# A macaron block with linear attention: the reciprocal denominators go to the channels by DMA and multiply A.v's output instead of q, the key sums of all groups stand in the scores' buffer, and the engines' orders are rewritten

## The reference

```
x = x + 0.5 * ffn(layernorm(x))
x = x + attn(layernorm(x))
x = x + 0.5 * ffn(layernorm(x))          # the same ffn weights

ffn:  s = x @ Win + bin            # 512 -> 64
      g = sum_i relu(s * W1[:, i] + b1[:, i]) * W2[:, i] + b2     # 16 inner units
      out = g @ Wout + bout        # 64 -> 512
attn: q, k, v = split(x @ w_attn)  # 512 -> 3 * 512, 16 heads of 32 channels
      q = elu(q) + 1;  k = elu(k) + 1
      S_t = S_{t-1} + k_t v_t^T;   z_t = z_{t-1} + k_t          # per head, causal
      y_t = (q_t S_t) / (q_t . z_t + 1e-6)
      out = y @ w_proj
```

## Time and profile before

| | |
|---|---|
| runs, median of 3 | 2411.91 us |
| profiled execution, its own time | 2411.75 us |
| its span | 2410.0 us |
| TensorE matmul busy | 2315.7 us (96%) |
| weight loads | 1796.5 us (75%) |
| VectorE, ScalarE, GpSimd busy | 79%, 59%, 34% |
| mean granted clock, share of full | 0.985 |

### The profile page before, as it was taken

How to read it: one execution, slowest core, us unless ns; L and a number is a source line. 1 busy time by engine, 2 the same in 40 slices (tenths; PEclk the granted TensorE clock), 3 DMA queues, 4 the chain that set the end, 5 groups by cost and what they waited for, 6 DMA issues and landing times.

```text
span 2410.0 us, 76110 instructions
## 1 busy us (share of the span) xinstructions
PE 2315.7 (96%) x33474; PEld 1796.5 (75%) x33474; DVE 1898.9 (79%) x3346; ACT 1424.5 (59%) x2267; POOL 824.3 (34%) x869
## 2 busy tenths in 40 slices
PE   3999999999999999999999999999999999999995
PEld 3777777777777777777777777777777777777774
DVE  6678887788887778887788887788878778887756
ACT  5556556556566556666556656555656655655644
POOL 6223333333333333333233333323233333333211
PEclk7999999999999999999999999999999999999997
DMA  5001101111101111101111100111100111100000
GB/s 171 1 2 36 35 4 37 37 37 37 37 2 37 36 37 37 37 2 37 37 37 37 37 18 21 37 37 37 37 20 19 37 37 37 36 20 2 19 19 36
DMA packets 39355, 76.98 MB, mean 32 GB/s; under 512 B 4081, under 2 KB 4081, under 8 KB 39026
## 3 DMA queue, kind: packets, MB, share of 16 engines
q1 hardware_dynamic: 39026, 72.12, 8.7%
HBM read 38.56 MB, written 33.55 MB: 30 GB/s over the span
## 4 chain that ended last, share of the span: by engine, by line
PE 67%; DVE 11%; POOL 8%; issue 5%; ACT 4%; DMA 3%; SPq 1%; DVEq 0%; POOLq 0%
PE bank L978 28%; PE att L978 14%; PE att L1081 5%; PE att L1106 5%; POOL z L347 4%; POOL res L339 3%; PE bank L1012 2%; PE att L1012 2%; PE att L996 2%; DVE z L721 2%; DVE st L649 2%; PE att L1097 2%; PE bank L1070 2%; PE att L1051 1%; PE bank L1021 1%
## 5 line engine op out<-in xcount | busy, mean ns | idle before, releaser
L439 ACT ACTIVATE xhat<-res,nmr,rstd 128x512 f32<-128x512 f32 x384 | 301.1, 808 | 287.4 <-DVE nmr L657 235.5
L454 ACT ACTIVATE ffr<-ffs,b1c,w1c 128x512 f32<-128x512 f32 (+1 forms) x544 | 425.5, 810 | 6.4 <-DVE acc_psum L684 3.2
L684 DVE SCALAR_TENSOR_TENSOR acc_psum<-ffr,w2c,acc_psum 128x512 f32<-128x512 f32 (+1 forms) x510 | 382.2, 750 | 33.7 <-ACT ffr L454 11.0
L351 POOL TENSOR_SCALAR_AFFINE_SELECT A<-A 128x512 f32<-128x512 f32 x256 | 157.1, 638 | 614.5 <-ACT A L416 614.5
L347 POOL TENSOR_TENSOR z<-qT,z 128x512 f32<-128x512 f32 x128 | 201.8, 1587 | 470.0 <-DVE zc L726 227.6
L339 POOL TENSOR_TENSOR res<-res,hbout 128x512 f32<-128x512 f32 x256 | 323.7, 1287 | 4.0 <-ACT xhat L439 3.4
L649 DVE BATCH_NORM_STATS2 st<-res 128x6 f32<-128x512 f32 x384 | 259.7, 676 | 20.5 <-DMA res<-in_L_attn_x_dram 15.2
L746 DVE TENSOR_TENSOR A<-att,tri 128x512 f32<-128x512 f32 x256 | 166.4, 681 | 58.2 <-PE att L1081 57.2
L978 PE MATMUL att<-xh,wa_h 128*128 128x512 f32 x524 | 207.0, 395 | 0.0
L978 PE MATMUL att<-xl,wa_h 128*128 128x512 f32 x524 | 207.0, 395 | 0.0
L978 PE MATMUL att<-xh,wa_l 128*128 128x512 f32 x524 | 207.0, 395 | 0.0
(11 more groups left out here) (129 smaller groups left out, 5133.1 us busy)
## 6 DMA issues: line engine op xcount, KB each, us to landing
res<-in_L_attn_x_dram SPq DMA_DIRECT2D x32, 1024.0 KB, 5.5
out_dram<-res SPq DMA_DIRECT2D x32, 1024.0 KB, 4.3
kT<-in_L_attn_w_attn_dram SPq DMA_DIRECT2D x1, 1024.0 KB, 5.3
qT<-in_L_attn_w_attn_dram SPq DMA_DIRECT2D x1, 1024.0 KB, 10.7
v<-in_L_attn_w_attn_dram SPq DMA_DIRECT2D x1, 1024.0 KB, 14.1
A<-in_L_attn_w_proj_dram SPq DMA_DIRECT2D x4, 256.0 KB, 13.1
win<-in_L_ffn_Win_dram SPq DMA_DIRECT2D x4, 128.0 KB, 8.0
z<-in_L_ffn_Wout_dram SPq DMA_DIRECT2D x2, 128.0 KB, 7.7
```

The source lines that it names most:

```text
L351: eng.affine_select(out=A[:, h, :, :], in_=A[:, h, :, :], compare_op=ALU.is_ge, fill=0.0, base=0, pattern=[[0, 4], [1, P]], channel_multip ...
L439: eng.activation(xhat[t % 2][:, :], res[b % SLOTS][:, t, :], ACT.Identity, bias=nmr[:, n, b % 2, t:t + 1], scale=rstd[:, n, b % 2, t:t + 1 ...
L454: eng.activation(ffr[i % 2][p, :], ffs[p, :], ACT.Relu, bias=b1c[p, i:i + 1], scale=w1c[p, i:i + 1]).then_inc(s_hr, 1)
L684: eng.scalar_tensor_tensor(psum[p, :], r[p, :], w2c[p, i:i + 1], psum[p, :], ALU.mult, ALU.add).then_inc(s_hm, 1)
```

## The change

- `spread` leaves TensorE, with `chans_of` and `qnorm`. SP now writes the reciprocals to a scratch tensor in DRAM (four DMAs of 16 x 128), waits for them, waits for this turn's `ff_in` and for `ynorm` of the block before, and reads them back with four DMAs, each of which puts 8 KB (4 heads x 512 tokens) into every one of a group's 32 partitions. They land in `rs`, which is the memory of `xf[1]`, the transposed input of the first ffn.
- `ynorm` (VectorE, four of them) multiplies A.v's output in `att` by `rs`, in place, before `ysplit`.
- `scores` waits for elu + 1 of q and k alone. The running sums of all four groups stand in `A` (`z4`) instead of two alternating buffers, so a `zsum` waits for no `den`; `score` and `mask`, which write `A`, wait for all of `den`.
- `ktok` has two halves, so a `key` copy waits for the `update` before the last.
- The orders of TensorE, VectorE, ScalarE and GpSimd, and the bank table, are rewritten.

```diff
+            def spread(b):                                  # SP
+                e.wait_ge(s_rec, b + 1)
+                for t in range(TILES):
+                    eng.dma_start(scratch[b % 2, :, t, :], rden[D * t:D * t + 16, :]).then_inc(s_rw, 16)
+                e.wait_ge(s_rw, 64 * (b + 1))
+                e.wait_ge(s_fi, b + 2)
+                e.wait_ge(s_yn, 4 * b)
+                for g in range(4):
+                    eng.dma_start(rs[D * g:D * g + D, :, :].rearrange("d h n -> d (h n)"),
+                                  scratch[b % 2, 4 * g:4 * g + 4].rearrange("h t n -> (h t n)").unsqueeze(0)
+                                  .to_broadcast([D, 4 * BLK])).then_inc(s_rs, 16)
...
-            def qnorm(b, t):                                # VectorE
-                w = slice(t * P, t * P + P)
-                e.wait_ge(s_rb, b + 1)
-                eng.tensor_tensor(qT[:, :, w], att[:, t, :].rearrange("p (g i) -> p g i", g=4), qT[:, :, w],
-                                  ALU.mult).then_inc(s_qn, 1)
+            def ynorm(b, t):
+                e.wait_ge(s_num, 4 * b + t + 1)
+                e.wait_ge(s_rs, 64 * (b + 1))
+                eng.tensor_tensor(att[:, :, 0:P], att[:, :, 0:P], rs[:, :, t * P:t * P + P], ALU.mult).then_inc(s_yn, 1)
...
-                e.wait_ge(s_den, 4 * b + g - 1)             # zsum, VectorE
+                e.wait_ge(s_num, 4 * b)
+                e.wait_ge(s_walo, 4)
...
-                e.wait_ge(s_qn, 4 * b + t + 1)              # scores, TensorE
+                for which in range(2):
+                    e.wait_ge(s_elu[which], 4 * b + 4)
...
-                e.wait_ge(s_num, 4 * b + t + 1)             # ysplit, ScalarE
+                e.wait_ge(s_yn, 4 * b + t + 1)
...
-                e.wait_ge(s_up, nth_update(b, t) - 1)       # key, ScalarE
+                e.wait_ge(s_up, nth_update(b, t) - 2)
```

More of the change, by code:

```diff
@@ L274, in _ @@
             load(4)
[L275 to L280, removed]
+            for j in range(NB + 1):
+                if on(j):
+                    spread(j)
+                if on(j - 1):
+                    store(j - 1)
+                    if on(j - 1 + SLOTS):
+                        load(j - 1 + SLOTS)
             for b in range(NB - SLOTS, NB):
@@ L394, in _ @@
                 if on(j - 1):
+                    bias(0, j - 1, 1)
+                    bias(0, j - 1, 2)
                     bias(0, j - 1, 3)
                 if on(j):
+                    mask(j, 3, 0)
                     mask(j, 3, 2)
[L398 to L404, removed]
                     rstds(L3, j)
@@ L629, in _ @@
                     channels(j + 1, 3)
-                if on(j) and updates(j, 3):
-                    key(j, 3)
                 if on(j):
@@ L872, in _ @@
                 if on(j - 1) or on(j + 2):
-                    hidden(j, 6)
+                    hidden(j, 7)
+                if on(j + 1):
+                    channels(j + 1, 0)
                 if on(j):
@@ L878, in _ @@
                 if on(j - 1) or on(j + 2):
-                    hidden(j, 7)
                     hidden(j, 8)
+                if on(j):
+                    update(j, 1)
+                    ynorm(j, 1)
+                if on(j - 1) or on(j + 2):
                     hidden(j, 9)
                 if on(j):
-                    update(j, 1)
                     ysplit(j, 1)
-                    outer(j, 0)
-                    mask(j, 2, 3)
-                    mask(j, 2, 1)
-                if on(j + 1):
-                    channels(j + 1, 0)
                 if on(j - 1) or on(j + 2):
@@ L910, in _ @@
                     ysplit(j, 3)
+                if on(j) and updates(j, 3):
+                    update(j, 3)
                 if on(j + 1):
                     channels(j + 1, 2)
-                if on(j + 3):
-                    shift(L1, j + 3)
-                if on(j):
-                    outer(j, 2)
-                if on(j + 1):
-                    channels(j + 1, 3)
                 if on(j - 1) or on(j + 2):
@@ L1157, in _ @@
                 if on(j):
-                    den(j, 0)
-                    den(j, 1)
-                    key(j, 0)
                     values(j, 1, 0)
@@ L1164, in _ @@
                 if on(j):
-                    den(j, 2)
-                    den(j, 3)
+                    key(j, 0)
                     values(j, 1, 1)
-                    spread(j)
+                    scores(j, 0)
                     values(j, 2, 0)
                     values(j, 2, 1)
-                    scores(j, 0)
-                    key(j, 1)
                     values(j, 3, 0)
                     attend(j, 0)
-                    update(j, 0)
-                    values(j, 3, 1)
-                    scores(j, 1)
-                    key(j, 2)
-                    outer(j, 0, 0)
-                    attend(j, 1)
-                    update(j, 1)
-                    outer(j, 0, 1)
-                    scores(j, 2)
                 if on(j + 1):
@@ L1186, in _ @@
                 if on(j):
-                    outer(j, 1, 0)
-                    attend(j, 2)
-                    update(j, 2)
-                    outer(j, 1, 1)
-                    scores(j, 3)
+                    values(j, 3, 1)
+                    key(j, 1)
+                    scores(j, 1)
+                    update(j, 0)
+                    update(j, 1)
+                    key(j, 2)
+                if on(j) and updates(j, 3):
+                    key(j, 3)
+                if on(j):
+                    attend(j, 1)
+                    outer(j, 0, 0)
                 if on(j + 1):
@@ L1194, in _ @@
                 if on(j):
+                    update(j, 2)
+                    scores(j, 2)
+                    outer(j, 0, 1)
+                    attend(j, 2)
+                    outer(j, 1, 0)
+                    outer(j, 1, 1)
+                    scores(j, 3)
                     outer(j, 2, 0)
                     attend(j, 3)
+                if on(j) and updates(j, 3):
+                    update(j, 3)
                 if on(j + 1):
```

298 lines of the change are left out of this document (154 added, 144 removed).

## The result

The changed kernel takes 2397.95 us in the median of four runs (2396.27 to 2399.12), the one before, run beside it, 2410.85. The ratio is 0.9943 (95% interval 0.9931 to 0.9955): 13 to 14 us faster. 38 us were forecast: the sign was right, the time lies at the very end of the range of the forecast (2355 to 2398), the size is little more than a third.

What follows compares the result with a forecast made beforehand. TensorE's sequence of work, busy 96% of the span, was taken as the bound. 2411.75 minus 67.3 us removed (35.2 + 17.6 + 8.4 + 6.1) plus 28.8 of new waits gave 2373 us, range 2355 to 2398.

Steps and rivals of the forecast that it cites:

- `spread`, 35.2: On TensorE: removing `spread` saves its 1.10 us from start to next start in each of 32 blocks, 35.2 us.
- The wait at `den`, 17.6 with 0.05 left: TensorE's wait for GpSimd at the last `den`: 0.55 us a block goes, 17.6 in all; 0.05 a block stays.
- The waits at `ff_in`, 8.4: In the first, second and last block: `ff_in`'s 2.28 us wait for k's elu goes, plus 1.6 of slow clock; 8.4 us.
- One change fewer, 6.1: On TensorE: one change from narrow to wide matmuls fewer a block, 0.19 us each, 6.1 us saved.
- `ynorm` and its chain, 0.1, 0.1 and 0.15: From A.v through `ynorm` to the low part: the next `scores` waits 0.1, 0.1 and 0.15 us at tiles 0 to 2.
- Masks: New TensorE waits for masks: tile 1 0.5 (odd) or 0.1 (even blocks), tile 3 0.15, tile 0 mean 0.1 us.
- The DMAs, nothing: Scratch write and read: the read takes 7.7 us of the 8.4 available, in time by 0.7, so its price is 0.
- A: Rival: the new waits on TensorE are hidden too, its own sequence is the bound, 2344 us; chance 0.12.
- B: Rival: new waits at the `ynorm` chain and masks eat the whole gain, 2411 us; chance 0.08.
- C: Rival: slow scratch reads land `rs` late, `ynorm` and `scores` wait, slower, spread between 2400 and 2520 us; chance 0.13.
- D: Rival: `scores` still hangs on `den` through `mask` and `score`, which costs nothing; under 1%.

Runs made afterwards that it cites:

- e5: The kernel before without the 32 matmuls of `spread` and without `qnorm`'s four multiplications, `scores` waiting for elu + 1 of q and k; 2367.13 us, ratio 0.9811.
- e3: The changed kernel with GpSimd's bias sums of the next block moved behind the fourth state sum; 2385.71 us, ratio 0.9886 to the kernel before.
- e8: e6 with `ynorm` multiplying only the first 4 of 128 columns of each bank, all waits and DMAs kept; 2369.5 us, ratio 0.9824 to the kernel before.
- e6: The changed kernel with bias sums behind the fourth state sum and 196 more TensorE instructions ahead of block 0; 2373.5 us, ratio 0.9839 to the kernel before.
- e1: The changed kernel with 196 more TensorE instructions (49 small matmuls) ahead of block 0; 2383.69 us, ratio 0.9879 to the kernel before.
- e2: The changed kernel with 64 more TensorE instructions (16 small matmuls) ahead of block 0; 2412.69 us, ratio 1.0003 to the kernel before.
- e9: The kernel before with the DRAM writes, reads and `ynorm` in place of `spread` and `qnorm`, all engines' old orders kept; 2605.52 us, ratio 1.0801.

## Why the prediction was right in sign and wrong in size

- **`spread`, 35.2.** Right. e5 gave 46: 35 for `spread`, 6 for the joined run, some 5 for gaps of the instruction supply that were gone too.
- **The wait at `den`, 17.6 with 0.05 left.** The step that failed first. The prediction gave the last scan no time of its own: it "ends earlier because k's last projection is now made before q's". In fact it stands beside the bias sums that the new order of GpSimd puts there, takes 2.0 to 2.3 us, and 0.50 or 0.22 us of wait stay: mean 0.36 for the 0.05. e3 gave back 14 us, of which this is 11. What runs beside the scan in the new order was not looked at. The 17.6 is also a little high, since it was read from an even block: in odd blocks the last `den` of before takes 1.13 for 1.25, which gives 15.7.
- **The waits at `ff_in`, 8.4.** Right: in the kernel after none of TensorE's waits there is for an elu, and turns 0 and 1 are 7.2 us shorter, 1.5 of it what every turn gained. But TensorE pays for the new order as it enters the loop, and no term had that: it waits 1.91 us for `xl` and starts at 63.93 for 61.89, and the granted clock, 0.50 until then in both, rose to 1.00 at 69.7 for 62.9. Its 5.8 us of matmuls at half the clock cost some 3 us, the late start 2: about 5 in all (an estimate).
- **One change fewer, 6.1.** The size of a change is right (e5), but part of what it gave went elsewhere: A.v followed by a transpose or by wide matmuls takes 1.01, followed by `update` 0.90 or 0.87, and the new order has more of the first kind.
- **`ynorm` and its chain, 0.1, 0.1 and 0.15.** The sum is about right, the reason is not. The transposes ahead of `scores` of tile 1, and those ahead of `update` and `scores` of tile 2, take 0.53 from start to start for 0.41, and there is nothing at tile 3. But the 0.12 stay in e8, where `ynorm` has 4 columns, and in the whole run of the kernel after `scores` waits for a low part twice, 1.0 us together: they belong to transposes with other small matmuls behind them. The chain itself costs about what e8 gave, some 0.1 a block for the 0.35; `ynorm` takes 0.70, for 0.75.
- **Masks.** The stretch ahead of tile 1's `attend` is 0.73 (odd) and 0.21 us (even) longer for 0.5 and 0.1 (the list of waits has 8.8 us in 18 for VectorE's mask, 0.5 each, as forecast; the rest is again transposes with small matmuls behind them); tile 0 0.43 in even blocks, a mean of 0.2 for 0.1; tile 3 0.08 for 0.15; tile 2 has 0.12 that I had left out. With both stalls gone (e6) the steady turn is 70.78, the 70.8 that was predicted.
- **The DMAs, nothing.** Right: in the block shown the reads landed 7.5 us after their issue, for 7.7, `ynorm` came 8.9 after it, for 8.4, and 1.4 us were to spare, for 0.7.
- **The step that was missing.** Nothing in the sum spoke of the supply of instructions: it stood at nothing without a reason. The trace of before showed it (three gaps of 0.9 to 1.1 us at one remainder by 256, at 243.6, 530.6 and 1541.7), and the number of instructions in a pair could be counted from the orders. It costs 14 us, the larger part of the error: -38 + 14 (supply) + 10 (`den`) = -14, as measured. e1 and e2 show it from both sides. That the sum closes so well is partly luck, and so is it that e6, without either, comes to the predicted 2373: some 5 us of before's own gaps went, which nobody forecast, and some 5 us at the entry of the loop came.
- **The rivals.** A and B are out: the steady turn is 71.1, between 69.9 and 72. C did not come; reads landing 1 to 2 us later would have made `ynorm` wait, and e9 shows what then happens. D is out: what `scores` waits for is those two low parts.

## What to carry to other kernels

A step that goes out of a loop changes not only the engines' time but the number of instructions a turn: if that comes near a multiple of 256, a bad place can last for many turns: count where the boundary falls, and try a few instructions more ahead of the loop before judging the change. When GpSimd's and VectorE's orders are rewritten, price each VectorE step beside what GpSimd does at that moment. A path through DRAM has to be judged in the order that it will run in: the same path was 14 us faster in one and 193 us slower in the other.

## What was not expected of the hardware

- **Supply of instructions.** TensorE stalled 0.8 to 2.2 us at numbers of one remainder by 256, where a boundary follows the one before it at some 3.2 to 4.0 us, the stall included. In the late turn shown they lie at 2095.89, 2099.24 and 2103.25, and the instruction queue's transfers began 0.9 to 1.1 us after each of them and took 0.9 to 1.4. In all eight gaps the late instruction started 1.4 to 1.6 us after the end of the last such transfer (in the 14 of e2 1.2 to 1.4). That a fetch must be back before the next boundary is passed is what this suggests; no run measured it by itself, and elsewhere in the run a transfer came later than its boundary by several us and nothing stalled (the boundary at 1240.76, the transfer at 1250.95). The Trainium skill (Runtime: NRT & Kernel Launch, Instruction fetch mechanics) states the blocks of 16 KiB, or 256 instructions, and calls the cost of crossing a boundary "mostly hidden". The size agrees with these runs; the cost does not, where small matmuls stand close: 14 us after, 30 in e2 against e1.
- **VectorE beside GpSimd.** A scan of 128 x 512 took 1.22 us alone and 2.07 beside a bias sum, and a pair of bias sums 3.49 instead of 2.6.
- **Copies from DRAM.** 1 MB in 8 KB rows, each read 32 times, landed in 6.5 to 8.4 us. From the first packet to the last it flowed at 163 to 222 GB/s, 192 in the median, near the 208 of w_proj's load into the same groups of partitions: reading one row 32 times cost little or nothing. The 13.1 us of that load are no measure, since it stood behind the three loads of `w_attn`, 1 MB each.
